# A causal mask added by VectorE and applied by GpSimd instead of by matmuls, and one-hots made by narrow comparisons

## The reference

```python
x = x + tanh(g_xattn[0]) * L0_xattn(layernorm(x), ctx, ctx, ...)   # 16 heads of 16, causal
x = x + tanh(g_ffn[0])   * L0_ffn(layernorm(x), ...)               # 32 experts, the best 8 of each token, 256 places each
x = x + tanh(g_xattn[1]) * L1_xattn(layernorm(x), ctx, ctx, ...)   # 16 heads, not causal
x = x + tanh(g_ffn[1])   * L1_ffn(layernorm(x), ...)               # 8 experts, the best 2, 1024 places each

# the causal attention of layer 0
scores = einsum('bhqd,bhkd->bhqk', wq, wk) / sqrt(Dh)
scores = where(tril, scores, finfo.min) + attention_mask
out = einsum('bhqk,bhkd->bhqd', softmax(scores), wv)
```

## Time and profile before

| | us |
|---|---|
| median of the three timed runs | 2217.09 |
| lowest and highest | 2213.77, 2218.43 |
| the profiled execution | 2205.22 |
| its span from first to last instruction | 2203.5 |
| PE busy | 1856.2 (84%) |
| VectorE (DVE) busy | 1102.1 (50%) |
| ScalarE (ACT) busy | 865.4 (39%) |
| GpSimd (POOL) busy | 676.7 (31%) |

### The profile page before, as it was taken

How to read it: one execution, slowest core, us unless ns; L and a number is a source line. 1 busy time by engine, 2 the same in 40 slices (tenths; PEclk the granted TensorE clock), 3 DMA queues, 4 the chain that set the end, 5 groups by cost and what they waited for, 6 DMA issues and landing times. The chain is left out here.

```text
span 2203.5 us, 30067 instructions
## 1 busy us (share of the span) xinstructions
PE 1856.2 (84%) x10491; PEld 1044.6 (47%) x10491; DVE 1102.1 (50%) x2800; ACT 865.4 (39%) x1780; POOL 676.7 (31%) x573
## 2 busy tenths in 40 slices
PE   2799898798884699945799999999881999999995
PEld 1345454454443577722334444433331566666664
DVE  3476676676744444431877777777611111212111
ACT  1256554464452222203277777765650111111110
POOL 1212322312223477732212312231113233333322
PEclk9899999999986799977899999999995999999998
DMA  3544353343122478833433334422112333333313
GB/s 92 159 125 153 111 168 102 113 130 124 55 71 71 128 171 172 169 54 107 141 92 112 101 89 128 123 87 76 41 39 87 85 75 75 75 77 75 70 28 96
DMA packets 204246, 222.86 MB, mean 101 GB/s; under 512 B 33439, under 2 KB 195232, under 8 KB 203432
## 3 DMA queue, kind: packets, MB, share of 16 engines
q1 hardware_dynamic: 176458, 177.48, 26.3%
q0 software_dynamic: 27648, 43.60, 10.7%
HBM read 155.06 MB, written 86.93 MB: 110 GB/s over the span
## 5 line engine op out<-in xcount | busy, mean ns | idle before, releaser
L829 DVE TENSOR_REDUCE nmx<-mxb 128x1 f32<-128x512 f32 (+3 forms) x1024 | 584.7, 586 | 253.3 <-PE mxb L667 128.7
L719 ACT ACTIVATE pt<-stb 128x512 f32<-128x512 f32 (+3 forms) x1024 | 500.9, 519 | 373.6 <-PE stb L680 217.4
L664 PE MATMUL mxb<-kst,qst 96*128 96x512 bf16 (+4 forms) x1024 | 354.8, 350 | 74.1 <-DVE nmx L829 63.1
L677 PE MATMUL stb<-qst,kst 99*128 99x512 bf16 (+4 forms) x1024 | 351.2, 349 | 11.1 <-ACT pt L719 7.9
L691 PE MATMUL ob<-pt,va 128*32 128x512 f32 (+3 forms) x2048 | 238.0, 537 | 1.2 <-ACT pt L719 1.1
L1411 PE MATMUL e_h_bank<-e_xT,e_w 128*128 128x512 f32 x512 | 224.9, 598 | 6.1 <-ACT e_xT L1451 5.4
L1425 PE MATMUL e_y_bank<-e_w,e_h 128*128 128x256 f32 x1024 | 226.9, 379 | 0.0
L677 PEld LDWEIGHTS stb<-qst,kst 102*128 102x128 bf16 (+1 forms) x1024 | 100.5, 99 | 238.1 <-ACT pt L719 147.0
L1425 PEld LDWEIGHTS e_y_bank<-e_w,e_h 128*128 128x128 f32 x1024 | 192.9, 190 | 31.8 <-issue 7.2
L1093 POOL TENSOR_TENSOR qk<-qk,parts 128x1024 f32<-128x1024 f32 x32 | 68.4, 2136 | 453.7 <-ACT qk L752 230.9
L664 PEld LDWEIGHTS mxb<-kst,qst 99*128 99x128 bf16 (+1 forms) x1024 | 101.2, 99 | 196.5 <-DVE nmx L829 134.1
(11 more groups left out here) (229 smaller groups left out, 2540.1 us busy)
## 6 DMA issues: line engine op xcount, KB each, us to landing
qk_parts<-parts SPq DMA_DIRECT2D x16, 1536.0 KB, 5.9
qst<-qk_parts SPq DMA_DIRECT2D x384, 64.0 KB, 2.3
kst<-qk_parts SPq DMA_DIRECT2D x384, 64.0 KB, 2.2
e_w<-in_L_ffn_w SPq DMA_DIRECT2D x16, 1024.0 KB
rows<-rows SPq DMA_DIRECT2D x15, 1060.0 KB, 8.6
crow<-in_ctx SPq DMA_DIRECT2D x16, 512.0 KB
x_after_l<-xres SPq DMA_DIRECT2D x16, 512.0 KB, 3.2
e_gu_nat<-in_L_ffn_gate_up_proj SPq DMA_DIRECT2D x64, 128.0 KB
```

The source lines that it names most:

```text
L664: last = pe.matmul(out[:, 0:nk], qst[par][0:rows_used, h, qt * P:(qt + 1) * P], kst[par][0:rows_used, h, 0:nk], start=True, stop=not causal)
L677: last = pe.matmul(out[:, q0:S], kst[par][0:ROWS, h, kt * P:(kt + 1) * P], qst[par][0:ROWS, h, q0:S], start=True, stop=not causal)
L719: act.activation(pt[:, u % 8, q_from(kt):S], stb[(STEPS * b + u) % N_ST][:, q_from(kt):S], ACT.Exp, scale=SCALE).then_inc(s["st_free"], 1)
L829: dve.tensor_reduce(nmx[:, qt, h:h + 1], mxb[(STEPS * n + u) % N_MX][:, 0:k_to(qt)], AX.X, ALU.max, negate=True).then_inc(s["max_free"], 1)
```

## The change

- The two tables become one, `hide`, of 128 x 512 elements in bf16: -2^100 where the column exceeds the row by more than 384. Its last 128 to 512 columns are the mask of a maximum.
- The mask matmuls of `maxima` and `scores` are left out (512 each).
- `maxima` on VectorE in layer 0 is a `tensor_tensor_reduce`: the bank plus `hide`, times -1, written to one of four new tiles `masked`, with the minimum of it accumulated into `nmx`. It waits for `max_full` and, before it writes `masked` again, for its own maximum of four steps earlier.
- The scores are no longer masked. After a group of four exponentials GpSimd runs `hide(b, g, kt)`: one `affine_select` over 4 x 128 elements of `pt`, which sets those above the diagonal to zero. `values` waits for it by the new semaphore `pt_rdy` instead of for `st_free`.
- `differ` and its tiles `lo_d`, `hi_d` go. `one_hot` waits for `idx_rdy` and makes `lo1` by 8 comparisons of 128 elements with a scalar of each token, and `hv` by 8 of 64 elements, all on VectorE, for every item; its steps are now 6, 13, 19 and 21.
- `rest` and `low` are two operations of 512 elements each instead of one of 1024.
- GpSimd's order is written by steps too: `low` of q at 5, `norm1` at 14, `rest` of k at 16, `low` of k at 22, `norm2` at 29, `rest` of q at 61, `hide` at every fourth. In layer 1 the quarters of the scatter stand at 0, 16, 18 and 24, so that the second is ahead of `rest` of k; before it was behind it.

```diff
@@ constants @@
-            pool.affine_select(out=c.hide_st[:, :], in_=c.hide_st[:, :], compare_op=ALU.is_ge, fill=HIDDEN,
-                               base=0, pattern=[[1, P]], channel_multiplier=-1)
-            pool.affine_select(out=c.hide_max[:, :], in_=c.hide_max[:, :], compare_op=ALU.is_ge, fill=HIDDEN,
-                               base=0, pattern=[[-1, P]], channel_multiplier=1).then_inc(tables, 1)
+            pool.affine_select(out=c.hide[:, :], in_=c.hide[:, :], compare_op=ALU.is_ge, fill=HIDDEN,
+                               base=S - P, pattern=[[-1, S]], channel_multiplier=1).then_inc(tables, 1)
@@ tensor: maxima @@
-                if causal:
-                    last = pe.matmul(out[:, nk - P:nk], c.identb[:, :], c.hide_max[:, :], start=False, stop=True)
@@ tensor: scores @@
-                if causal:
-                    last = pe.matmul(out[:, q0:q0 + P], c.identb[:, :], c.hide_st[:, :], start=False, stop=True)
@@ tensor: values @@
-                pe.wait_ge(s["st_free"], STEPS * b + 16 * g + 4 * kt + 4)
+                if causal:
+                    pe.wait_ge(s["pt_rdy"], 16 * b + 4 * g + kt + 1)
+                else:
+                    pe.wait_ge(s["st_free"], STEPS * b + 16 * g + 4 * kt + 4)
@@ vector: maxima @@
-                dve.tensor_reduce(nmx[:, qt, h:h + 1], mxb[(STEPS * n + u) % N_MX][:, 0:k_to(qt)], AX.X, ALU.max,
-                                  negate=True).then_inc(s["max_free"], 1)
+                got = mxb[(STEPS * n + u) % N_MX][:, 0:k_to(qt)]
+                if causal:
+                    wait(dve, s["max_free"], STEPS * n + u - 3)
+                    dve.tensor_tensor_reduce(out=masked[u % 4][:, 0:k_to(qt)], in0=got, in1=c.hide[:, S - k_to(qt):S], scale=-1.0,
+                                             scalar=LARGEST, op0=ALU.add, op1=ALU.min,
+                                             accum_out=nmx[:, qt, h:h + 1]).then_inc(s["max_free"], 1)
+                else:
+                    dve.tensor_reduce(nmx[:, qt, h:h + 1], got, AX.X, ALU.max, negate=True).then_inc(s["max_free"], 1)
@@ vector: one_hot @@
+                dve.wait_ge(s["idx_rdy"], b + 1)
                 wait(dve, full["list"], 4 * b + t - 1)
-                    dve.wait_ge(s["apart_rdy"], apart(b, t))
-                    dve.tensor_scalar(lo1[t % 2][:, :, :], lo_d[t % 2][:, :, :], 0.0, None, ALU.is_equal)
-                    dve.tensor_scalar(hv[t % 2][:, :, :], hi_d[t % 2][:, :, :], 0.0, c.tok1[:, 0:1],
-                                      ALU.is_equal, ALU.mult).then_inc(s["lo_rdy"], 1)
+                for k in range(8):
+                    dve.tensor_scalar(lo1[t % 2][:, k, :], c.lanes[:, :], lo_f[:, t, k:k + 1], None, ALU.is_equal)
+                for k in range(8):
+                    last = dve.tensor_scalar(hv[t % 2][:, k, :], c.lanes[:, 0:N_HI], hi_f[:, t, k:k + 1], c.tok1[:, 0:1],
+                                             ALU.is_equal, ALU.mult)
+                last.then_inc(s["lo_rdy"], 1)
@@ gpsimd @@
             def rest(n, side):
-                src = qk[:, side, :, :]
-                pool.tensor_tensor(src, src, parts[:, side, 0, :, :], ALU.subtract).then_inc(s[("rest_q", "rest_k")[side]], 1)
+                for cc in range(NC):
+                    last = pool.tensor_tensor(qk[:, side, cc, :], qk[:, side, cc, :], parts[:, side, 0, cc, :], ALU.subtract)
+                last.then_inc(s[("rest_q", "rest_k")[side]], 1)
+            def hide(b, g, kt):
+                pool.wait_ge(s["st_free"], STEPS * b + 16 * g + 4 * kt + 4)
+                seen = pt[:, 4 * (kt % 2):4 * (kt % 2) + 4, kt * P:(kt + 1) * P]
+                pool.affine_select(out=seen, in_=seen, compare_op=ALU.is_ge, fill=0.0, base=0, pattern=[[0, 4], [1, P]],
+                                   channel_multiplier=-1).then_inc(s["pt_rdy"], 1)
-            def differ(b, t):
-                pool.tensor_tensor(lo_d[t % 2][:, :, :], c.lanes[:, :].unsqueeze(1).to_broadcast([P, 8, P]),
-                                   lo_f[:, t, :].unsqueeze(2).to_broadcast([P, 8, P]), ALU.subtract)
-                pool.tensor_tensor(hi_d[t % 2][:, :, :], c.lanes[:, 0:N_HI].unsqueeze(1).to_broadcast([P, 8, N_HI]),
-                                   hi_f[:, t, :].unsqueeze(2).to_broadcast([P, 8, N_HI]), ALU.subtract).then_inc(s["apart_rdy"], 1)
+                for u in range(STEPS):
+                    if layer and done is not None and u in (0, 16, 18, 24):
+                        quarter = (0, 16, 18, 24).index(u)
+                        scatter(done, NSCAT // 4 * quarter, NSCAT // 4 * (quarter + 1))
+                    if causal and cur is not None and u % 4 == 3:
+                        hide(cur, u // 16, u % 16 // 4)
+                    if u == 5 and nn is not None:
+                        low(nn, 0)
+                    if u == 14 and n3 is not None:
+                        norm1(n3)
+                    if u == 16 and nn is not None:
+                        rest(nn, 1)
+                    if u == 22 and nn is not None:
+                        low(nn, 1)
+                    if u == 29 and prev is not None:
+                        norm2(prev)
+                    if u == 61 and n3 is not None:
+                        rest(n3, 0)
```

72 lines of the change are left out of this document (15 added, 57 removed).

## The result

| | before | after |
|---|---|---|
| median of the timed runs, us | 2215.4 (2204.6 to 2218.4) | 2189.6 (2188.9 to 2190.8) |
| ratio to before | 1 | 0.9893 (0.9858 to 0.9927) |
| profiled run: span, us | 2203.5 | 2187.2 |
| first maxima to last scores of layer 0, us | 591.1 | 569.2 |
| first maxima to the token list, us | 648.7 | 626.1 |

A forecast was written before the change was run, and what follows sets the result against it. PE was taken to bound passes without one-hots, the GpSimd-VectorE exchange to add to the others. Gains of 53 + 10 + 9 + 2 + 9 = 83 us from 2217 gave 2134 us, range 2098 to 2178.

The forecast's parts named there:

- What bounds the kernel: Layer 0 attention: PE bounds passes without one-hots; the exchange between GpSimd and VectorE adds to those with them.
- One-hots, the step that failed: One-hot groups on VectorE: 16 narrow comparisons at 0.10 and 0.085 us, 1.5 us a group, 6.0 a pass.
- narrow comparisons are dear: Rival for the one-hot groups: 0.2 us each or held by selections, 54 us more, time 2188 us; chance 0.08.
- four passes: Layer 0 passes with full one-hot work, 239.4 to 552.3 us: 260 us in place of 312.9, a gain of 53.
- pass at 552 us: Layer 0 pass with one-hots but little GpSimd work: from 64.2 to 55 us, a gain of 9.
- Mask matmuls: PE in layer 0: 128 fewer matmuls a pass at 0.055 us, 7.0 us, nearly all on the path where PE bounds.
- Maxima: VectorE in layer 0: adding the mask costs 0.06 us a maximum, 3.8 us a pass.
- half-rate rival: Rival for VectorE's maxima: the accumulating maximum runs at half rate, 21 us more a pass, time 2255 us; chance 0.08.
- Selections: GpSimd zeroing the triangle between exponentials and values matmuls: 0.8 us each, hidden in passes with maxima, 8 us lost in the last.
- selections come late: Rival for GpSimd's queue: a selection takes 1.2 us behind long operations, some 40 us, time 2174 us; chance 0.12.
- The sum of quarters: A pass with one-hots by the longer engine per quarter plus waits: 18.5, 17.5, 15.5 and 13.5, together 65.0 us.
- VectorE above 90% of a pass: Sign in the layer 0 passes: VectorE's share rising above 90% would show the prediction wrong.

The follow-up runs named there:

- The mask alone: The changed kernel with the one-hots of before put back (two GpSimd subtractions, two wide VectorE comparisons a group); ratio 1.0028.
- the one-hots alone: The kernel before with only the one-hots changed, to narrow comparisons on VectorE, the mask staying with the matmuls; ratio 0.9855.
- with constants: The changed kernel with constants in place of the operands per partition in all 16 comparisons of a group, so the experts' lists stay empty; ratio 0.9654.
- selections aside: The changed kernel with GpSimd's selections made on a tile nobody reads, the values matmuls waiting for the exponentials alone; ratio 0.9878.

## Why the prediction failed, point by point

*What bounds the kernel.* Right: PE in the passes without one-hots, the exchange with GpSimd in the others. The mask alone and the one-hots alone show which of the two the gain hangs on.

*One-hots, the step that failed.* "8 of 128 elements at 0.10 and 8 of 64 at 0.085 make 1.5 us a group" was read off small operations without an operand per partition. The sizes were right to 2% (0.102 and 0.086 with constants); the operands were not counted, 0.06 us each, 24 in a group, 1.45 us. The group takes 2.96 us alone, and 3.3 in the median of the passes. This is the rival "narrow comparisons are dear", forecast with 0.2 us each, 1.7 us more a group, 54 us and 2188 us; I gave it 0.08, and it came; its 0.2 us each was a bound without a reason, and that it meets the measured mean of 0.185 is luck. By the terms of the sum (us; profiled runs):

| term | forecast | measured | with constants |
|---|---|---|---|
| four passes (312.9 before) | -53 | -20.3 | -53.0 |
| first pass | 0 | +2.8 | +0.6 |
| second and third pass | -5, -5 | 0.0, -4.0 | -0.1, -4.0 |
| pass at 552 us | -9 | +0.2 | -4.7 |
| last pass | -2 | -0.6 | -4.3 |
| last scores to the list | -9 | -0.7 | -8.0 |
| together | -83 | -22.6 | -73.5 |

With the price of the comparisons put right by the run with constants, 51 of the 60 missing microseconds of layer 0 return. That its four passes meet the forecast to 0.1 us is partly luck: two errors there cancel, 3.8 us a pass counted for the maxima and nearly nothing measured, and nothing counted for the selections, which are worth 2.0 a pass (292.6 against 284.4 us for the four).

*Mask matmuls.* 7.0 us of PE a pass was right (62.9 to 56.1 busy). "In a pass that PE bounds nearly all of it is on the path" was too much: 4.0 in the third pass and 3.3 to 4.1 without one-hots, since PE now waits for VectorE's banks and the selections. In the passes with dear comparisons it is nothing, because VectorE sets the first two quarters. In the second pass the granted clock goes with the missing 5: 0.91 and 55.9 us there, 1.00 and 51.6 to 52.2 us in the three kernels with no selections, with selections aside and with the plain maximum. What takes it down in the one and not in the others isn't shown.

*Maxima.* Forecast 0.06 us each, measured 0.008 to 0.015 from start to start, and nothing that the time shows: with the plain maximum the four passes take 292.7 us, with the mask 292.6. The half-rate rival is out: 687 ns for 512 elements.

*Selections.* 0.64 us for the 0.8 assumed. "In a pass with maxima it is hidden" failed: PE's direct waits were as small as said, 1.1 us a pass, but the selections hold VectorE's operations, which I had put down only under the dear comparisons. Together 26 us (14 to 38, by the two intervals), 17 in the profiled stretch; the rival "selections come late" named 40 by waiting, of which there were about 5. Slowed VectorE work explains 11 to 12 of the 17. In the last pass, without cover, PE waited 3.7 us for them, forecast 8.

*The sum of quarters.* Its form was right, VectorE's work plus 1.6 us where VectorE is longer: with the comparisons at the assumed price the medians of its quarters are 18.3, 17.6, 15.7 and 13.1 for 18.5, 17.5, 15.5 and 13.5.

*What was to show it.* I had named VectorE above 90% of a pass as the sign of a wrong prediction. It was at 81% (59.6 of 73.3 us), and 85% in the first two quarters: PE and VectorE wait for each other through two banks, so a sign of 90% was set too high. The distance between the comparisons (0.1 forecast, 0.162 and 0.206 seen) was the sign that spoke. The other sign named, PE's idle time before the values matmuls, did grow: 12.5 us in the whole run, before 1.2.

*What stays open:* the pass at 552 us is 4 us longer than forecast even with constants, and why isn't shown. How much of the comparisons' price goes through PE's clock isn't separated, nor what GpSimd's halved operations and new order do by themselves; the traces show only that VectorE is slowed beside them too (8.8 us in the stretch without selections, and 39.5 beside GpSimd's work in the kernel before). The first maxima of the changed kernel start 1.6 us later, but among the kernels here they start anywhere from 76.2 to 79.8 us, so that needs no cause of its own.

## What to carry to other kernels

Price an instruction by rows with the same kinds of operands, not only of the same size: a wide operation with broadcast inputs was cheaper (2.13 us) than 16 narrow ones with operands per partition (2.96), although each narrow one looked nearly free. A forecast that comes out right in one term can hide two errors: compare each term, not the sum. When work is taken from the engine that bounds, ask in each stretch whether it still bounds afterwards; a saving and a cure of another wait don't add up, and may cancel. Split a change into the half that costs next to nothing elsewhere and the half that pays for it on another engine: with wide one-hots the first was worth 15 us, and the second lost 12.

## What the runs showed of the hardware

- An operand per partition costs a narrow VectorE operation 0.06 us: starts 0.086 us apart with none, 0.146 with one, 0.206 with two (64 elements), 0.102 and 0.162 (128 elements).
- The maximum with a second tensor, a copy written out and an accumulator takes 687 ns for 512 elements, like the plain one (688 in the kernel of the one-hots alone); the 82 ns read of the accumulator runs beside the next operation's start.
- A GpSimd selection of 4 x 128 f32 elements in place takes 0.637 us; beside such a selection alone VectorE comparisons of 0.25 to 0.29 us took up to 0.73 and 0.76, beside the halves of `rest` (some 1.15 us each) up to 1.23, and beside the undivided `rest` (2.17 us, the kernel of the one-hots alone) 2.12.
- The maxima, which read one operand from PSUM, kept their length beside GpSimd: 687 ns for 512 elements with the selections and 688 without.
- The Trainium skill (VectorE: DVE Perf Modes, section on the TRN2 errata) gives 58 cycles and a quarter of the elements, an estimate of 0.094 and 0.077 us as in the prediction; the starts with constants come near it (0.102, 0.086), and those with operands per partition show what it leaves out.
